# A graph network on one core: TensorE's signals in the chunk loops moved from the product to a drain behind it

## The reference

```
# first network, per layer (L = 4, HEADS = 8, HID = 128)
q = (h @ Wq.T + bq)[dst];  k = (h @ Wk.T + bk)[src];  v = (h @ Wv.T + bv)[src]
alpha = sum(q * k, -1) / 4                       # 16 values per head
ex = exp(alpha - segment_max(alpha, dst)[dst])
out = segment_sum(ex / denom[dst] * v, dst)      # denom = segment_sum(ex, dst)
h = gated mix of out and h @ Ws.T, layer norm, feed-forward with gelu, residual
# second network
rbf = exp(-(dist - centers)**2 / (2 * width**2))         # 16 basis values
msg = silu([x[src], x[dst], rbf] @ mw1 + mb1) @ mw2 + mb2
out = mlp([x, segment_mean(msg, dst)]), layer norm
x = layernorm(x + out)                           # after each network
```

## Time and profile before

| | |
|---|---|
| timed runs, median of 3 | 5616.35 us (5614.72 to 5620.73) |
| profiled execution, span | 7840.1 us |
| PE busy | 4625.7 us (59%) |
| DVE busy | 4037.4 us (51%) |
| POOL busy | 3849.3 us (49%) |
| ACT busy | 2769.9 us (35%) |

### The profile page before, as it was taken

How to read it: one execution, slowest core, us unless ns; L and a number is a source line. 1 busy time by engine, 2 the same in 40 slices (tenths; PEclk the granted TensorE clock), 3 DMA queues, 4 the chain that set the end, 5 groups by cost and what they waited for, 6 DMA issues and landing times.

```text
span 7840.1 us, 106032 instructions
## 1 busy us (share of the span) xinstructions
PE 4625.7 (59%) x22831; PEld 3727.9 (48%) x22832; DVE 4037.4 (51%) x11107; ACT 2769.9 (35%) x6493; POOL 3849.3 (49%) x4066
## 2 busy tenths in 40 slices
PE   4555555655556556555555565555555656666667
PEld 2444444534444445344444453444444545555555
DVE  4555555645555556455555565555555553333334
ACT  1333333423333334233333342333333432323333
POOL 3555555335555553345555543455555425555553
PEclk6666666676666666766666667666666677877887
DMA  5222222222322222222223222222322211111111
GB/s 127 78 79 76 77 76 78 52 66 73 79 78 77 78 80 56 69 67 79 76 78 79 78 62 69 68 78 77 80 78 79 60 33 43 44 44 44 44 44 30
DMA packets 267188, 536.13 MB, mean 68 GB/s; under 512 B 116253, under 2 KB 148689, under 8 KB 266509
## 3 DMA queue, kind: packets, MB, share of 16 engines
q0 software_dynamic: 180992, 490.24, 23.6%
q1 hardware_dynamic: 78901, 35.89, 1.9%
q10 hardware_dynamic: 6936, 6.69, 0.3%
HBM read 512.41 MB, written 18.03 MB: 68 GB/s over the span
## 4 chain that ended last, share of the span: by engine, by line
PE 26%; another core or an unknown queue 26%; issue 20%; DVE 17%; ACT 5%; DVEq 4%; ACTq 1%; SPq 0%; DMA 0%; POOL 0%; POOLq 0%
PE bank L806 9%; PE bank L825 7%; DVE acc L1265 6%; ACT oh L556 2%; DVEq L333 2%; PE bank L797 2%; PE bank L851 2%; PE bank L810 1%; DVE alpha L1288 1%; PE bank L879 1%; DVEq L1265 1%; DVE slots L1361 1%; DVE oh L1249 1%; PE bank L1001 1%
## 5 line engine op out<-in xcount | busy, mean ns | idle before, releaser
L508 POOL DMA_INDIRECT slots<-kv_table,idx x3224 | 3065.2, 951 | 3133.0 <-PE bank L825 1275.8
L825 PE MATMUL bank<-slots,oh 128*128 128x136 f32 (+1 forms) x8060 | 1593.0, 351 | 569.1 <-DVE acc L1265 506.4
L806 PE MATMUL bank<-qs,ohT 128*128 x8080 | 1685.7, 356 | 235.1 <-ACT ohT L547 129.2
L825 PEld LDWEIGHTS bank<-slots,oh 128*128 128x128 f32 x8060 | 1411.7, 252 | 704.7 <-DVE acc L1265 608.2
L806 PEld LDWEIGHTS bank<-qs,ohT 128*128 128x128 f32 x8080 | 1434.4, 257 | 456.6 <-issue 434.4
L1265 DVE TENSOR_TENSOR acc<-acc,bank 128x136 f32 (+1 forms) x4030 | 1172.0, 291 | 614.6 <-PE bank L825 171.5
L1282 DVE TENSOR_TENSOR slots<-slots,bank 128x512 f32<-128x512 f32 x808 | 551.8, 683 | 1322.6 <-remote 1291.5
L547 ACT ACTIVATE ohT<-bank,miss 128x512 f32<-128x512 f32 x1010 | 676.7, 683 | 1367.9 <-PE bank L797 1234.5
L508 POOL DMA_INDIRECT slots<-src_table,idx x806 | 760.4, 943 | 756.9 <-DMA idx<-src_e 247.9
L843 PE MATMUL bank<-ident,alpha 128*128 128x128 f32 x204 | 93.7, 459 | 1487.2 <-DVE alpha L1288 1481.7
L556 ACT ACTIVATE oh<-iota,rel_e 128x128 f32<-128x128 f32 x3168 | 962.8, 387 | 0.0
(11 more groups left out here) (257 smaller groups left out, 4079.5 us busy)
## 6 DMA issues: line engine op xcount, KB each, us to landing
slots<-kv_table,idx POOLq DMA_INDIRECT x3224
kv_table<-slots SPq DMA_DIRECT2D x20, 660.0 KB, 3.4
slots<-src_table,idx POOLq DMA_INDIRECT x806
resets<-flat_len ACTq DMA_DIRECT2D x51, 128.0 KB
idx<-src_e SPq DMA_DIRECT2D x255, 8.0 KB
terms<-flat_rel SPq DMA_DIRECT2D x255, 12.0 KB
resets<-flat_rst SPq DMA_DIRECT2D x2, 1551.0 KB
w<-in_w SPq DMA_DIRECT2D x8, 256.0 KB
```

The source lines that it names most:

```text
L508: pool.indirect_dma_start(slots[:, k, t, 0:width], None, table, bass.IndirectOffsetOnAxis(ap=idx[:, k, t:t + 1], axis=0))\
L806: mm = pe.matmul(o, ohT[:, j % 2, t, :], qs[:, blocks[j * G + t], 0:HID], start=True, stop=basis is None)
L825: mm = pe.matmul(bank[6 + part % 2][:, o:o + width], oh[:, k % 2, t, :], slots[:, k, t, HID:HID + width], start=True, stop=True)
```

## The change

In all the functions that the chunk loops call, the increment is taken off the matmul, and a `drain` instruction on PE carries it. The waits, the order of the products and all other engines stay. Matmuls in the setup and in the node stages keep their increments. An example of each kind:

```
@@ spread_terms
-                pe.matmul(bank[j % 2][:, :], spread[:, j, :], terms[:, k, :], start=True, stop=True)\
-                    .then_inc(sq_spread, counts_for(j, groups))
+                pe.matmul(bank[j % 2][:, :], spread[:, j, :], terms[:, k, :], start=True, stop=True)
+                pe.drain().then_inc(sq_spread, counts_for(j, groups))
@@ rows
-                mm.then_inc(q_spread, counts_for(j, groups))
+                pe.drain().then_inc(q_spread, counts_for(j, groups))
@@ add_up
                     if t % G == G - 1 or (last and t == LAST_PLACES - 1):
-                        mm.then_inc(slot_free[k][j], 1)
+                        pe.drain().then_inc(slot_free[k][j], 1)
                     elif t == end - 1:
-                        mm.then_inc(part_ps, len(WITHIN) if last else 1)
+                        pe.drain().then_inc(part_ps, len(WITHIN) if last else 1)
@@ turn_alpha
-                pe.transpose(bank[4][:, 0:P], alpha[:, :, :].rearrange("p h t -> p (h t)"), ident[:, :])\
-                    .then_inc(alpha_turned, 1)
+                pe.transpose(bank[4][:, 0:P], alpha[:, :, :].rearrange("p h t -> p (h t)"), ident[:, :])
+                pe.drain().then_inc(alpha_turned, 1)
...
```

## The result

| | median | lowest to highest | runs |
|---|---|---|---|
| before | 5616.53 us | 5614.72 to 5620.73 | 4 |
| after | 8278.80 us | 8239.98 to 8302.38 | 4 |

The ratio is 1.4729, 95% interval 1.4683 to 1.4775: 2662 us slower. The forecast was 6800 us with a range of 6000 to 7700. The direction was right, but the loss is more than twice the 1184 us forecast, and the time lies outside the range. The profiled execution of the kernel after took 8257.2 us with a span of 8255.4 us. Unlike the profile of before, it agrees with its timed runs.

What follows compares the result with a forecast made beforehand. It took PE and DVE, alternating in one chain with little idle time, to bound the kernel. 5616 + 1000 (attention) + 220 (messages) = 6836, less 40 us for gathers: 6800 us, range 6000 to 7700.

Steps and rivals of the forecast that it cites:

- the sum for the attention chunk: Three stretches of an attention chunk, 3.7 + 0.1 + 1.1 = 4.9 us, times 204 = 1000 us.
- of the 3.8 us 2.65 are covered: From the ends to the next `ex`: nine drains cost 3.8 us, PE's idle time hides 2.65, leaving +1.1 us.
- quick chunk: Chunk at the end of each attention layer, its gathers all issued: 18.9 us, against 28.0 for the others in that profile.
- the signs that were named: Profile after: 5055 drains, 0.4 us gaps, alpha 13 us after `ex`, shorter wait for `ex`, last chunks near 24 us.
- A timed chunk is the quick one: Timed runs have nearly no stalls; with 18.9 us attention chunks throughout, the profile comes within 18 us of the timed median.
- that rival: POOL's gathers, 20.0 us a chunk, already bind, so some drains are free: 6460 us; chance 0.06.
- late signals: Rival: product increments come late in rows 3 and drains deliver them at once, 510 us gained: 5400 us; chance 0.04.
- The count: Product groups that carry a signal, each getting a drain: 5055, 21 in a full attention chunk, 16 in a message step.
- The price of one drain: PE's lost time at each drain behind a product: 0.42 us, bounds 0.17 and 0.70.
- cheap drain: Rival: a drain on PE loses only the overlap of successive products, 0.17 us: about 5900 us; chance 0.14.
- colder clock: Rival: more gaps bring PE's clock to 0.6, 8.7 us a chunk and 7 a step: 7750 us; chance 0.14.
- The message step: Message loop: 16 drains cost 6.7 us, 2.4 us of idle time covers part, +4.3 us, times 51 = 220 us.

Runs made afterwards that it cites:

- the `pow` run: Kernel before with one small `pow` and a drain on POOL ahead of each group of four gathers: 8126.03 us, ratio 1.4464.
- the clean one: Second profiled execution of the unchanged kernel before: 5621.04 us, span 5619.2 us.
- the pair with rows twice: Every row product issued twice, the first result overwritten, on the kernel after (8314.24 us) and on the kernel before (5814.63 us).

## Why the prediction was wrong

The direction and the count were right, and the price of a stop nearly so. Two steps failed, and both are terms of the sum for the attention chunk, forecast at +4.9 us and measured at +11.6. One is the cover: "of the 3.8 us 2.65 are covered", where only some 0.6 us were. The other is the spacing of the products, which the forecast left as in a quick chunk, at nothing; the colder clock makes it some 4 us, by an estimate below. Of the signs that were named, the 5055 drains, the gap of 0.4 us ahead of rows and the end of PE's wait for `ex` came. But alpha is turned 17.1 us after `ex` and not 13, and the chunk from 1646.2 to 1678.5 us, behind the last gather of its layer, takes 32.3 us and not 24. That last number also shows that the gathers don't hold the kernel after.

**What bounds the kernel.** "A timed chunk is the quick one" fell. The timed chunk is the gathers' (19.7 us, 64% of the chain on POOL, and the `pow` run). That by itself would have led the other way: it makes some drains free, as the 0.14 us each of `add_up` alone shows, and it would have lowered the forecast, to 6460. So the miss has its cause elsewhere. The argument against that rival took the waits for the tables (477.3 and 168.7 us) from the stretched execution; in the clean one they are 344.3 and 124.7, and 4030 x 1.25 + 469 = 5507 us lies below the timed median. The idea that late signals were to be won or lost is void too: those waits were of one execution, and a bare drain costs the same as a signalling one.

**The count** of 5055 was right.

**The price of one drain**, 0.42 us, was nearly right: 0.38 between two parts of `add_up` at full clock, 0.54 at half clock, and 0.495 on average in the pair with rows twice, all within the 0.17 to 0.70 given. Its two parts are in the timeline: a gap of 0.21 to 0.43, and the tail of the last product, which the next used to overlap. The rival "cheap drain" (0.17) is out. The Trainium skill, page "VectorE: DVE Perf Modes", section "The DRAIN you can't avoid", gives the boilerplate drains, which stand in the preamble and postamble, as about 12 ns. Behind a matmul this case doesn't show that price: by it the estimate was 61 us for all 5055, and the runs show 2662.

**The three stretches of the attention chunk.** Means over all chunks, of the clean profile of before and of after:

| stretch | before | after | grew by | predicted |
|---|---|---|---|---|
| `ex` to alpha | 10.3 | 17.1 | 6.8 | 3.7 |
| alpha to ends | 1.5 | 1.4 | -0.1 | 0.1 |
| ends to `ex` | 7.9 | 12.8 | 4.9 | 1.1 |

The sum is 11.6 us against 4.9. The third stretch is the worst miss, and the step that failed there is "of the 3.8 us 2.65 are covered". The argument was that DVE is last there and PE has idle time, 0.34 for `ohT` and 2.31 for `ex`. But the way from the ends to `ex` runs from DVE through PE ("cols"), ACT, DVE, PE again (`shift`) and ACT, where `ex` stands behind the `scale` that needs `shift`. PE's idle time ahead of `ex` lies behind those two products and covers nothing in front of them. The means show it: from the ends to the product of `shift` the chunk grows by 5.4 us, from 5.8 to 11.3 and more than the 3.8 of all nine drains, and only from there to `ex` does it get shorter, from 2.1 to 1.5. And 2.31 us was one chunk's idle time; in the clean profile of before the mean is 1.2. The timeline of the kernel after, from the ends to `ex`:

```profile
1034.79 1.27 PE L825 MATMUL bank<-slots,oh 128*128 128x136 f32 x4 [0.21 <-issue]
1034.87 0.22 DVE L1326 TENSOR_SCALAR shift<-gap,resets 1x8 f32<-1x8 f32 x1 [0.15 <-DVE gap L1323]
...
1037.58 0.60 PE L797 MATMUL bank<-terms,spread 12*128 12x512 bf16 x1 [1.52 <-issue]
...
1038.93 0.56 PE L866 MATMUL bank<-ones,c_row 1*128 1x1 f32 x2
1039.55 0.16 ACT L578 COPY icol<-bank 128x2 f32<-128x2 f32 x1 [0.55 <-PEq L867]
...
1039.75 0.48 DVE L1339 TENSOR_TENSOR_SCAN fwd<-resets,icol,bank 128x128 f32<-128x128 f32 x1 [2.70 <-ACT icol L578]
...
1041.03 0.29 DVE L1347 TENSOR_TENSOR bwd<-bank,fwd 128x128 f32<-128x128 f32 x1
...
1043.15 0.59 PE L874 MATMUL bank<-shift,oh 128*128 128x8 f32 x2 [0.35 <-issue]
1043.79 0.18 ACT L583 ACTIVATE scale<-bank 128x8 f32<-128x8 f32 x1 [2.74 <-PEq L875]
...
1044.15 0.31 ACT L586 ACTIVATE ex<-bwd 128x128 f32<-128x128 f32 x1 [0.18 <-issue]
```

DVE had its shift ready at 1035.09 but gets `icol` at 1039.71, since "cols" stands behind four products, a drain, bare register loads (1.52 us) and a spread with its drain. Over the kernel that scan of DVE waits 550.1 us for `icol`; in the clean profile of before that wait is 5.6. `scale` is late once more for `shift` (2.74 us), and `ex` with it: DVE had its input ready at 1041.32, and ACT starts it at 1044.15, behind `scale`. Here nearly every drain counts.

**The clock.** This is the second step that failed: the forecast kept products at the spacing of a quick chunk. In the first stretch shown, 18.28 us against 9.56, the eleven stops are 3.43 us of gaps and 11 x (0.48 - 0.23) = 2.75 us of tails at half clock, 6.2 us or 0.56 each, inside the bounds of the price. The other 2.5 us of the growth, and the wait for alpha that went, are the wider spacing of the products themselves, 0.11 us for each that had been at full clock. The attention clock fell from 0.74 to 0.53. A longer chunk with the same products lowers it too, but less: in the run with the `pow` the chunk takes 29.9 us and the clock is 0.64. What the clock costs in all can only be estimated, and two ways give about the same. The first: 32 further matmuls at full-clock spacing are 32 x 0.11 = 3.5 us, and the chunk with them was 0.6 us shorter, so at the higher clock the chunk after would be some 27 us, and about 4 us of the 11.6 are the clock's. The second: between the two levels, a mean of 0.74 is 52% of the time at the lower one and 0.53 is 94%, and 0.42 x 80 matmuls in a chunk x 0.11 us = 3.7 us. With the 2 us of cover that wasn't there, that is 6 of the 6.7 us that the forecast lacks; the rest isn't divided here.

The rival "colder clock" had the mechanism and the clock (0.6, measured 0.60), at 0.14, but only 1.3 us of spacing in a chunk. It counted a fall of 0.15 in the mean clock as 0.15 of the time at the lower level, where it is 0.30, and attention alone fell further than the mean. (It also took 86 products; the earlier trace rows has 162 in two chunks, and the traces show 80 in one.) With its 8.7 us a chunk it came closest, at 7750 us. The Trainium skill, page "TensorE: Matmul & The Clock Gate", section "A second HAM failure mode: psum-queue depth-cycling", reports that short idle times between groups of matmuls can make the clock swing between half and full. This case agrees where stops stand behind rows (0.67, 0.59, 0.53, 0.50 in the table, and up again when each group of rows was given more products); with drains behind `add_up` alone the clock stayed at 0.77.

**The message step** was put at +4.3 us. From the last attention scan to the end the kernel takes 305.7 us more (1465.2 against 1159.5), 6.0 for each of 51 steps. But a timed step had been held by the gathers at 20.1 us. Against the 17.0 of a quick step, from which the forecast started, the 26.2 us after are 9.2 more, which is above the 6.7 of all sixteen drains with no cover at all. How that divides between cover, price and clock stays open.

**Where the loss lies:** 200 attention chunk periods x 11.66 us + 305.7 us = 2638 us, against 8255.4 - 5619.2 = 2636 us between the two spans, so nothing outside the chunk loops grew. The forecast's own price of a drain with no cover at all, 5055 x 0.42 = 2120 us, would have been closer than the forecast. How the 11.6 us divide between stops and clock stays an estimate, since no run here held the clock and changed nothing else.

## What to carry over

A drain behind a matmul is a full stop of TensorE, some 0.4 us at full clock and more at half clock here, and it also bares the register loads behind it; put the increment on the matmul. Idle time of an engine covers added delay only if it lies behind that delay and ahead of the next hand-over: follow a chain that returns to the engine several times product by product. If a profile is far from the timed runs, take a second one before anything is built on it, and price a change that adds gaps at the lower clock, with the neighbouring edits in place and not one by one.

## What was not expected of the hardware

- The costs of drains do more than add up: the 2015 of `add_up` cost 0.14 us each alone and 0.85 each beside the other 3040.
- 2015 drains behind `add_up` alone raised the mean clock, from 0.77 to 0.80, and 3040 behind the rest lowered it to 0.72.
- 8080 more matmuls cost 35 us in the kernel with drains, as the clock rose from 0.60 to 0.78, and 197 us in the one without (0.77 to 0.85).
- On GpSimd a drain with a 1.20 us operation between gathers costs 2.48 us, as the next gather starts 1.52 us after it and not 0.30.
- One execution of the kernel before took 7840 us with waits of up to 8.1 us for matmuls that had long ended, and none of its timed ones (5610.06 to 5629.61 us) did; the cause stays open.
